# A two-layer graph network on one core: the layout of the degree histogram's one-hots, and how the first feature table is made and handed over

## Chip, cores and metric

One core of a Trainium2 chip. The metric is the device time of one execution in microseconds (us); lower is better. PE is TensorE, DVE VectorE, ACT ScalarE, POOL GpSimd, SP SyncE. PEld is TensorE's loading of weights, which overlaps its matmuls.

## What is computed

12,500 nodes with 32 features and 212,500 edges sorted by destination go through two message-passing layers. The part that the change touches stands ahead of the first layer:

```python
h = jnp.maximum(_layernorm(x, axis=-1), 0.0)
deg_out = jax.ops.segment_sum(ones, src, num_segments=n)
norm_src = jax.lax.rsqrt(jnp.maximum(deg_out, 1.0))
h = features * norm_src[:, None]
msgs = h[src]
agg = jax.ops.segment_sum(msgs, dst, num_segments=n)
```

So each node's outgoing edges are counted, its normalised features are scaled with the inverse root of that count, and layer 1 gathers these scaled rows edge by edge and sums them by destination. Layer 2 computes an edge network (32 to 64 to 256), combines it with gathered node rows and sums again; the change doesn't touch it.

## The kernel before

**Tiling.** Nodes are padded to 12,800 and lie as 128 partitions x 100 rows, in 25 blocks of 4 rows a partition (BLOCKS, BR, NR). Edges are padded to 208 chunks of 1,024, which are 8 tiles of 128 edges. A ring of four buffers (RING) holds the indices (idx) and the gathered rows (g) of four chunks.

**The degree histogram.** Each source node is split in two digits: one of 128 (dig_p) and one of 100 (dig_r), as bfloat16, with an edge tile's 128 edges on the partitions. The 1,664 tiles are taken in 104 batches of HB = 16 tiles. For a batch DVE compares the digits with a constant ramp (iota_p, iota_r) and writes two one-hot arrays (L842 to L852): oh_p holds for each tile 128 flags, oh_r 100 flags. Both are stored with the tile index innermost, 16 tiles side by side, so that one tile's flags lie 16 elements (32 bytes) apart. Each array is written in four pieces (PIECES) that split the 128 or the 100 flags: 8 DVE instructions a batch. TensorE then multiplies, tile by tile, the 128x128 one-hot (as weights) with the 128x100 one-hot and adds up all 1,664 products in one PSUM region (L580 to L591):

```python
mm = pe.matmul(deg, oh_p[:, b, :, t], oh_r[:, b, :, t], start=False, stop=False,
               skip_group_check=True)
```

There are two buffers for the one-hots. DVE waits ahead of batch n until TensorE has signalled the end of batch n-2 (hist_used, L845), and TensorE waits for hist_ready (L582).

**Beside it** POOL gathers rows of the unscaled features for the first 32 chunks (256 indirect DMAs of 128 rows, L445 to L447) and ACT copies them aside (keep, L473). SP loads the indices of the next four chunks as ring buffers come free (load0, L330).

**The table.** When all tiles are counted, DVE takes the inverse root (L861 to L863) and computes hn, the scaled features of all nodes, in one instruction (L864). ACT writes it to DRAM as table1 in one DMA (L486, L487). POOL waits for that (L450) and gathers from it. SP in the meantime has a list of its own (L356 to L371): it waits for bounds_done, the least and greatest destination of each chunk, which DVE reduces after hn (L870, L871); sends these bounds to DRAM and back, broadcast over the partitions; waits for whole_clear; then loads the indices for the first gathers of table1 (load0(EARLY_ITERS - 1), L365); then waits for table1_out and loads a second, local copy of the table (whole, L368, L370).

**After it** DVE clears the accumulator (L874), shifts the destinations (L877) and makes the registers' rows (L880 to L892). Then layer 1 runs: DVE makes a chunk's destination one-hots (L895), TensorE multiplies them with the gathered rows (L600), and DVE adds the sums (L907) when TensorE has signalled. POOL may gather into a ring buffer again when DVE has made the one-hots of a later chunk (used_in, L436).

Of the kernel before, what the change touches and what calls it, by code (L numbers as in the profile page):

```python
# [26 lines left out]
ALU = mybir.AluOpType  # L27
# [6 lines left out]
P = 128  # L34
N_NODES, N_EDGES = 12500, 212500
FEAT, HID, MUL = 32, 64, 8
# [21 lines left out]
EPS = 1e-5  # L58
ALPHA, C110, SI_SCALE = 0.25, 1.0 / np.sqrt(3.0), 1.0 / np.sqrt(float(MUL))
HB = 16  # L60
PIECES = 4
HBATCH = CHUNKS * TILES // HB
EARLY_LINKS = 6
MID_LINKS = 24
MW = 56
# [7 lines left out]
def gnn_program(nc, x_rows, src_all, src_chunks, src_rows, dst_all, dst_chunks, edge_t, sh_chunks,  # L73
                w_l0, b_l0, w1, b1, w2, skip_w, sel_a, sel_b, ident_in, out):
    assert EARLY % RING == 0 and REG_ITERS > A_ITERS + 1
    assert CHUNKS % (2 * HB // TILES) == 0 and CHUNKS % 2 == 0
    with ExitStack() as ctx:
        def sb(name, shape, dt=F32):
# [53 lines left out]
        o = 0  # L132
        dig_p = msg_b[:, :, :, :].rearrange("p b t k -> p (b t k)").bitcast(BF16)[:, 0:T_ALL]
        dig_r, o = hist[:, o:o + T_ALL], o + T_ALL
        oh_p, o = hist[:, o:o + 2 * P * HB].rearrange("p (b j t) -> p b j t", b=2, t=HB), o + 2 * P * HB
        oh_r, o = hist[:, o:o + 2 * NR * HB].rearrange("p (b j t) -> p b j t", b=2, t=HB), o + 2 * NR * HB
        zero_b, o = hist[:, o:o + P], o + P
        early_at = -(-o // 2)
        early = acc_b[:, early_at:early_at + EARLY * TILES * FEAT]
        assert early_at + EARLY * TILES * FEAT <= ACC_W  # L140
        iotas = prod_a[:, :, :, :].rearrange("p b t k -> p (b t k)").bitcast(BF16)
        iota_p = iotas[:, 0:P * HB].rearrange("p (j t) -> p j t", t=HB)
        iota_r = iotas[:, P * HB:(P + NR) * HB].rearrange("p (j t) -> p j t", t=HB)

        dst_i, src_i, src_p, src_b, src_r = (acc_a[:, k * T_ALL:(k + 1) * T_ALL].bitcast(I32) for k in range(5))

# [81 lines left out]
        def by_block(dram):  # L228

            return dram.rearrange("(b p r) f -> p b r f", p=P, r=BR)  # L230
# [79 lines left out]
        def _(sp):  # L310
# [44 lines left out]

            sp.dma_start(early_src, src_rows[0:1, :].to_broadcast([P, CHUNK])).then_inc(early_src_in, 16)  # L356

            sp.wait_ge(bounds_done, 2)
            for k in range(2):
                sp.dma_start(bounds[k:k + 1, :].rearrange("a (q s) -> (a q) s", s=2), mm_c[:, k, :]).then_inc(bounds_out, 16)  # L360
# [1 line left out]
            for k in range(2):  # L362
                sp.dma_start(bound[:, k, :], bounds[k:k + 1, :].to_broadcast([P, CHUNKS])).then_inc(bounds_in, 16)
            sp.wait_ge(whole_clear, 1)
            load0(EARLY_ITERS - 1)  # L365
            sp.wait_ge(table1_out, 16)
            full = GROUPS - 1
            sp.dma_start(whole[:, 0:full, :], table1[0:full * P * GROUP, :].rearrange(  # L368
                "(k p b) f -> p k (b f)", p=P, b=GROUP)).then_inc(whole_in, 16)
# [42 lines left out]
        @block.gpsimd  # L412
        def _(pool):
            pool.iota(iota_all[:, :], [[1, P]], base=0, channel_multiplier=0,
                      allow_small_or_imprecise_dtypes=True).then_inc(iota_done, 1)
            pool.iota(part[:, :], [[1, 1]], base=0, channel_multiplier=1,
                      allow_small_or_imprecise_dtypes=True).then_inc(iota_done, 1)

            def gather(i, table, iteration, free, tiles=TILES):

                for j in range(RING):
                    pool.wait_ge(idx_in[j], 16 * (iteration + 1))
                    free(RING * i + j, j)

                    pool.sem_inc(slots_opened, 1)
                    for t in range(tiles):
                        pool.indirect_dma_start(  # L427
                            out=g[:, j, t, 0:FEAT], out_offset=None, in_=table,
                            in_offset=bass.IndirectOffsetOnAxis(ap=idx[:, j, t:t + 1], axis=0),
                        ).then_inc(gathered[j], 16)  # L430

            def kept_four_before(c, j):

                wait(pool, kept, c - RING + 1)

            def used_in(first_unit, per_iteration, position):  # L436


                def free(i):
                    return lambda c, j: pool.wait_ge(  # L440
                        onehot1_ready, first_unit + per_iteration * i + position[j] + 3)
                return free


            gather(0, x_rows, 0, kept_four_before)  # L445
            with pool.Fori(1, EARLY_ITERS) as i:
                gather(i, x_rows, i, kept_four_before)  # L447


            pool.wait_ge(table1_out, 16)  # L450
            gather(EARLY_ITERS, table1, EARLY_ITERS, kept_four_before)
            beside = used_in(0, len(UNITS), [UNITS.index((0, j)) for j in range(RING)])
            alone = used_in(A_UNITS, RING, range(RING))
            with pool.Fori(0, A_ITERS - 1) as i:
                gather(i, table1, i + (EARLY_ITERS + 1), beside(i))
            gather(A_ITERS - 1, table1, A_ITERS + EARLY_ITERS, beside(A_ITERS - 1), taken(True))
            with pool.Fori(0, REG_ITERS - A_ITERS - 1) as i:
                gather(i, table1, i + (EARLY_ITERS + 1 + A_ITERS), alone(i), taken(True))

            pool.wait_ge(table2_out, 16 * BLOCKS)
            over_iterations(pool, lambda i: gather(
                i, table2, i + ITERS, lambda c, j: wait(pool, d_ready, c - RING + 1)))

        @block.scalar
        def _(act):
# [14 lines left out]
                keep(i)  # L483
            square_root(2)

            act.wait_ge(table1_ready, 1)  # L486
            act.dma_start(by_block(table1), blocks_of(hn)).then_inc(table1_out, 16)  # L487
            keep(EARLY_ITERS - 1)

            def next_sources(e):  # L490
# [81 lines left out]
        def _(pe):  # L572
# [7 lines left out]
            def count(i):  # L580
                for b in range(2):
                    pe.wait_ge(hist_ready, 2 * i + b + 1)  # L582
                    for t in range(HB):
                        mm = pe.matmul(deg, oh_p[:, b, :, t], oh_r[:, b, :, t], start=False, stop=False,  # L584
                                       skip_group_check=True)
                    mm.then_inc(hist_used, 1)

# [176 lines left out]
        def _(dve):  # L764
# [53 lines left out]

            dve.wait_ge(iota_done, 2)
            for iota, m in ((iota_p, P), (iota_r, NR)):  # L820
                link(dve.tensor_copy(iota, iota_all[:, 0:m, None].to_broadcast([P, m, HB])))


            dve.wait_ge(x_loaded, 16)
# [17 lines left out]
            def count(i):  # L842
                for b in range(2):
                    n = 2 * i + b
                    wait(dve, hist_used, n - 1)  # L845
                    for iota, dig, oh, m in ((iota_p, dig_p, oh_p, P), (iota_r, dig_r, oh_r, NR)):
                        for part_m in range(0, m, m // PIECES):
                            rows_m = slice(part_m, part_m + m // PIECES)
                            ins = dve.tensor_tensor(oh[:, b, rows_m, :], iota[:, rows_m, :],  # L849
                                                    dig[:, None, bass.ds(n * HB, HB)].to_broadcast([P, m // PIECES, HB]),  # L850
                                                    ALU.is_equal)
                    ins.then_inc(hist_ready, 1)  # L852

            count(0)
            with dve.Fori(1, HBATCH // 2) as i:
# [5 lines left out]
            link(dve.tensor_scalar(stat[:, 1, :], ps[:, H_BANK, 0:NR], 1.0, None, ALU.max))  # L861
            rsqrt(stat[:, 1, :], norm_src[:, :])
            link(dve.tensor_tensor(norm_src[:, :], norm_src[:, :], stat[:, 2, :], ALU.mult))  # L863
            dve.scalar_tensor_tensor(out=hn[:, :, :], in0=xc[:, :, :], scalar=0.0, in1=rows(norm_src[:, :], FEAT),  # L864
                                     op0=ALU.max, op1=ALU.mult).then_inc(table1_ready, 1)
            dve.memset(whole[:, GROUPS - 1, :], 0.0).then_inc(whole_clear, 1)


# [223 lines left out]
            with dve.Fori(1, A_ITERS) as i:  # L1092
                beside_early(i)
            dve.wait_ge(par_loaded, 16 * N_PARAMS)
            dve.wait_ge(table1_out, 16)
            dve.wait_ge(whole_in, 32)
            link(dve.tensor_copy(split[0], whole))
            link(dve.tensor_tensor(whole, whole, split[0], ALU.subtract))
# [192 lines left out]
```

## Time and profile before

| | us |
|---|---|
| median of three runs | 6182.4 |
| fastest, slowest | 6169.01, 6199.66 |
| the profiled execution's own time | 6176.81 |
| its span (first to last instruction) | 6175.0 |
| PE busy / DVE busy / POOL busy | 3868.4 / 3197.1 / 3114.7 |
| ACT busy | 739.8 |

No engine is busy through the span. The stages in order: start and centring up to about 36 us, the histogram up to 653 us, the table and the bounds up to 690 us, layer 1 up to about 3100 us, layer 2 to the end. A busy share is an average over stages with different limits, so the share of the whole span tells little about the first 690 us. In the views "issue" is idle time that waited for nothing the profile shows, and "remote" is a wait whose releaser the profile does not name.

### The profile page before, as it was taken

To read this page: it belongs to the slowest core of one execution; us is meant where nothing else is said; L and a number is where in the kernel's file an instruction comes from. 1 tells how busy PE (TensorE), PEld (TensorE's weight loads), DVE (VectorE), ACT (ScalarE), POOL (GpSimd) and SP (SyncE) were. 2 spreads that over 40 slices of the span, in tenths; PEclk is the share of its full clock that TensorE was granted. 3 is DMA by queue.
4 is the path that set the end of the run, shared out by engine and by line. 5 is a ranking of instruction groups with operands and counts; after the bars stand their busy time and mean duration, and the time that the engine had idled before them with its cause. 6 is when DMAs were issued, how large, how long until landed. Compare 5 with 4: busy or idle time off the path is not lost.

```text
span 6175.0 us, 73355 instructions
## 1 busy us (share of the span) xinstructions
PE 3868.4 (63%) x19374; PEld 2580.2 (42%) x19375; DVE 3197.1 (52%) x6090; ACT 739.8 (12%) x2428; POOL 3114.7 (50%) x3222
## 2 busy tenths in 40 slices
PE   1069333333455556566667887778877887777877
PEld 0047332332222223222335555555555555555555
DVE  2058432332444334333346666666666766666666
ACT  0000000000000000000022222222222222222222
POOL 7710455555444454455545555554555555555553
PEclk9999955555677777777767787887787777887888
DMA  1100111111000000000001111110111111111110
GB/s 41 16 3 0 37 30 27 29 27 27 20 15 14 14 16 14 14 15 15 15 17 21 20 21 20 20 20 19 21 19 20 21 21 20 21 21 19 20 20 13
DMA packets 237464, 120.99 MB, mean 20 GB/s; under 512 B 148880, under 2 KB 224721, under 8 KB 237329
## 3 DMA queue, kind: packets, MB, share of 16 engines
q0 software_dynamic: 102912, 52.90, 5.9%
q1 hardware_dynamic: 123241, 48.20, 3.3%
q10 hardware_dynamic: 11280, 19.53, 1.0%
q8 instruction: 12, 0.20, 0.0%
q14 instruction: 19, 0.16, 0.0%
HBM read 115.44 MB, written 4.92 MB: 19 GB/s over the span
## 4 chain that ended last, share of the span: by engine, by line
PE 35%; another core or an unknown queue 34%; issue 13%; DVE 11%; DVEq 5%; ACT 2%; ACTq 0%
PE ps L719 11%; PE ps L600 8%; PE ps L707 5%; PE ps L584 5%; PE ps L634 2%; DVEq L912 2%; DVE prod_a L948 2%; DVE prod_a L957 2%; DVEq L911 1%; PE ps L622 1%; PE ps L666 1%; PE ps L753 1%; PE ps L755 1%; ACT q L552 1%
## 5 line engine op out<-in xcount | busy, mean ns | idle before, releaser
L427 POOL DMA_INDIRECT g<-table,idx x2960 | 2855.8, 965 | 2922.0 <-DMA idx<-src_chunks 992.8
L719 PE MATMUL ps<-w_s,hid 128*128 128x256 f32 x3328 | 1084.1, 478 | 353.6 <-ACT hid L540 281.0
L719 PEld LDWEIGHTS ps<-w_s,hid 128*128 128x128 f32 x3328 | 749.4, 237 | 900.9 <-issue 425.4
L907 DVE TENSOR_TENSOR acc_a<-acc_a,ps 33x68 f32 (+1 forms) x416 | 91.4, 220 | 1653.2 <-remote 1448.8
L1152 DVE TENSOR_REDUCE msg_b<-prod_b 128x128 f32<-128x1024 f32 x416 | 828.1, 1991 | 0.0
L634 PE MATMUL ps<-split_s,prod_a 128*128 128x512 bf16 x1568 | 574.7, 452 | 123.1 <-DVE prod_a L948 79.7
L540 ACT ACTIVATE hid<-ps,b_s 64x512 f32<-64x512 f32 x416 | 283.1, 681 | 2321.7 <-remote 1365.2
L707 PE MATMUL ps<-ef,w_s 32*64 32x512 f32 x832 | 527.0, 713 | 45.6 <-issue 42.9
L1136 DVE TENSOR_TENSOR prod_b<-ps,q 128x768 f32<-128x768 f32 x416 | 395.3, 950 | 287.5 <-remote 228.8
L584 PE MATMUL ps<-acc_b 128*128 128x100 bf16 x1664 | 317.7, 371 | 333.6 <-DVE acc_b L849 230.1
L600 PE MATMUL ps<-onehot,g 128*33 128x68 f32 x2816 | 275.9, 271 | 362.9 <-issue 168.5
L600 PEld LDWEIGHTS ps<-onehot,prod_a 128*128 128x128 f32 x3328 | 447.1, 210 | 82.6 <-issue 67.0
L600 PE MATMUL ps<-onehot,prod_a 128*128 128x68 f32 x3328 | 439.9, 290 | 45.6 <-issue 41.0
L600 PEld LDWEIGHTS ps<-onehot,g 128*33 128x33 f32 x2816 | 239.9, 142 | 447.4 <-issue 252.1
L584 PEld LDWEIGHTS ps<-acc_b 128*128 128x128 bf16 x1664 | 239.4, 148 | 411.7 <-DVE acc_b L849 243.2
L600 PE MATMUL ps<-onehot,msg_b 128*56 128x68 f32 x3328 | 289.1, 237 | 194.3 <-issue 193.8
L634 PE MATMUL ps<-xc,prod_a 128*128 128x512 bf16 x784 | 348.1, 444 | 46.3 <-issue 46.3
L552 ACT ACTIVATE q<-g,sh 128x32 f32<-128x32 f32 x1664 | 372.9, 309 | 0.0
L895 DVE TENSOR_TENSOR onehot<-iota_all,dst_rel 128x544 f32<-128x544 f32 x416 | 300.1, 722 | 65.2 <-issue 54.7
L600 PEld LDWEIGHTS ps<-onehot,msg_b 128*56 128x56 f32 x3328 | 239.6, 139 | 217.9 <-issue 202.6
L849 DVE TENSOR_TENSOR acc_b<-prod_a,msg_b 128x512 bf16<-128x512 bf16 x416 | 149.1, 421 | 350.1 <-remote 261.7
L634 PEld LDWEIGHTS ps<-split_s,prod_a 128*128 128x128 bf16 x1568 | 165.1, 111 | 351.1 <-issue 171.6
(127 smaller groups left out, 2949.2 us busy)
## 6 DMA issues: line engine op xcount, KB each, us to landing
g<-table,idx POOLq DMA_INDIRECT x2960
ef<-edge_t SPq DMA_DIRECT2D x208, 128.0 KB
ef<-src_rows ACTq DMA_DIRECT2D x31, 512.0 KB
prod_b<-src_rows SPq DMA_DIRECT2D x112, 64.0 KB
idx<-src_chunks SPq DMA_DIRECT2D x416, 4.0 KB
g<-x_rows,idx POOLq DMA_INDIRECT x256
sh<-sh_chunks SPq DMA_DIRECT2D x208, 16.0 KB
table<-hn ACTq DMA_DIRECT2D x1, 1600.0 KB, 7.3
```

Source lines behind the costliest of these rows:

```text
L427: pool.indirect_dma_start(out=g[:, j, t, 0:FEAT], out_offset=None, in_=table, in_offset=bass.IndirectOffsetOnAxis(ap=idx[:, j, t:t + 1], a ...
L540: act.activation(hid[0:HID, h, :], ps[0:HID, H_BANK + h, :], ACT.Relu, bias=b1_s[:, 0:1]).then_inc(hidden_ready, 1)
L552: act.activation(q[:, j % 2, t, 8:40], g[:, j, t, 0:FEAT], ACT.Copy, scale=sh[:, j, t, 0:1])
L584: mm = pe.matmul(deg, oh_p[:, b, :, t], oh_r[:, b, :, t], start=False, stop=False, skip_group_check=True)
L600: mm = pe.matmul(ps[0:m, S_BANK + b, col:col + WIN], r, oh(t), start=(t == 0), stop=(t == TILES - 1))
L634: mm = pe.matmul(ps[:, R_BANK + b, :], source[:, b, k, :], split[n][:, k, :], start=(k == 0 and n == 0), stop=(k == GROUPS - 1 and n == 2))
L707: pe.matmul(ps[0:HID, H_BANK + h, :], w1_s[32 * j:32 * j + 32, :], ef[32 * j:32 * j + 32, 512 * h:512 * h + 512], start=True, stop=True, t ...
L719: mm = pe.matmul(w_ps[h][:, t, :], hid[:, h, P * t:P * t + P], w2_s[:, :], start=True, stop=True)
L849: ins = dve.tensor_tensor(oh[:, b, rows_m, :], iota[:, rows_m, :], dig[:, None, bass.ds(n * HB, HB)].to_broadcast([P, m // PIECES, HB]), A ...
L895: dve.tensor_tensor(onehot[:, b, :, :], iota_all[:, None, 0:WIN].to_broadcast([P, TILES, WIN]), dst_rel[:, bass.ds(c * TILES, TILES)][:, : ...
L1136: dve.tensor_tensor(prod_b[:, h, :, 0:3, :].rearrange("p t m (i o) -> p t m i o", o=MUL), w[:, :, 128:192].rearrange("p t (i o) -> p t i o ...
L1152: dve.tensor_reduce(msg_b[:, b, 4 * h:4 * h + 4, 0:32].rearrange("p t (g o) -> p t g o", o=MUL), prod_b[:, h, :, :, :].rearrange("p t g (i ...
```

## The change

Three things are edited. One: the one-hots keep their 16 tiles a batch, but as four groups (QUADS) of QUAD = 4 tiles, with only the four tiles innermost; a tile's flags are now 4 elements (8 bytes) apart. The four DVE instructions for an array split the tiles and not the flags, and the ramps shrink to 4 copies of each value. Two: hn is computed in five instructions of 5 blocks each, ACT writes each part with a DMA of its own, and the waits for table1_out are for all five. Three: SP's load0(EARLY_ITERS - 1) moves ahead of the wait for the bounds.

```diff
-PIECES = 4
+QUAD = 4
+QUADS = HB // QUAD
+TABLE_PARTS = 5
+PART_BLOCKS = BLOCKS // TABLE_PARTS
-        oh_p, o = hist[:, o:o + 2 * P * HB].rearrange("p (b j t) -> p b j t", b=2, t=HB), o + 2 * P * HB
+        oh_p, o = hist[:, o:o + 2 * P * HB].rearrange("p (b q j t) -> p b q j t", b=2, q=QUADS, t=QUAD), o + 2 * P * HB
...
-        iota_p = iotas[:, 0:P * HB].rearrange("p (j t) -> p j t", t=HB)
+        iota_p = iotas[:, 0:P * QUAD].rearrange("p (j t) -> p j t", t=QUAD)
...
+            load0(EARLY_ITERS - 1)
             sp.wait_ge(bounds_done, 2)
...
             sp.wait_ge(whole_clear, 1)
-            load0(EARLY_ITERS - 1)
-            sp.wait_ge(table1_out, 16)
+            sp.wait_ge(table1_out, 16 * TABLE_PARTS)
...
-            act.wait_ge(table1_ready, 1)
-            act.dma_start(by_block(table1), blocks_of(hn)).then_inc(table1_out, 16)
+            for k in range(TABLE_PARTS):
+                part_b = slice(k * PART_BLOCKS, (k + 1) * PART_BLOCKS)
+                act.wait_ge(table1_ready, k + 1)
+                act.dma_start(by_block(table1)[:, part_b, :, :], blocks_of(hn)[:, part_b, :, :]).then_inc(table1_out, 16)
...
-                        mm = pe.matmul(deg, oh_p[:, b, :, t], oh_r[:, b, :, t], start=False, stop=False,
+                        mm = pe.matmul(deg, oh_p[:, b, t // QUAD, :, t % QUAD],
+                                       oh_r[:, b, t // QUAD, :, t % QUAD], start=False, stop=False,
                                        skip_group_check=True)
...
-                        for part_m in range(0, m, m // PIECES):
-                            rows_m = slice(part_m, part_m + m // PIECES)
-                            ins = dve.tensor_tensor(oh[:, b, rows_m, :], iota[:, rows_m, :],
-                                                    dig[:, None, bass.ds(n * HB, HB)].to_broadcast([P, m // PIECES, HB]),
-                                                    ALU.is_equal)
+                        for k in range(QUADS):
+                            ins = dve.tensor_tensor(
+                                oh[:, b, k, :, :], iota,
+                                dig[:, None, bass.ds(n * HB + k * QUAD, QUAD)].to_broadcast([P, m, QUAD]),
+                                ALU.is_equal)
...
-            dve.scalar_tensor_tensor(out=hn[:, :, :], in0=xc[:, :, :], scalar=0.0, in1=rows(norm_src[:, :], FEAT),
-                                     op0=ALU.max, op1=ALU.mult).then_inc(table1_ready, 1)
+            for k in range(TABLE_PARTS):
+                part_r = slice(k * PART_BLOCKS * BR, (k + 1) * PART_BLOCKS * BR)
+                dve.scalar_tensor_tensor(
+                    out=hn[:, part_r, :], in0=xc[:, part_r, :], scalar=0.0,
+                    in1=norm_src[:, part_r, None].to_broadcast([P, PART_BLOCKS * BR, FEAT]),
+                    op0=ALU.max, op1=ALU.mult).then_inc(table1_ready, 1)
```

The other waits for table1_out (L451 on POOL, L1095 on DVE) are changed in the same way, and oh_r and iota_r as oh_p and iota_p.

## Rows read from the trace of the kernel before

**Rows 1.** The page's slices: busy tenths of the span in 40 slices

```profile
PE   1069333333455556566667887778877887777877
DVE  2058432332444334333346666666666766666666
```

**Rows 2.** Stretches: length, busy us of PE, PEld, DVE, ACT, POOL, clock, DMA share, GB/s

```profile
36.00:372.00 336.00, 36.44 (x183) 26.17 (x184) 31.48 (x100) 10.84 (x26) 231.37 (x237) 1.00 0.09 14
372.00:653.00 281.00, 281.00 (x1483) 213.27 (x1482) 232.40 (x733) 0.00 (x0) 0.00 (x0) 1.00 0.00 0
```

**Rows 3.** Instruction groups from 372 to 653: busy us, mean ns, idle before

```profile
L584 PE MATMUL ps<-acc_b 128*128 128x100 bf16 x1483 | 281.6, 371 | 0.0
L584 PEld LDWEIGHTS ps<-acc_b 128*128 128x128 bf16 x1481 | 213.3, 148 | 67.7 <-DVE acc_b L849 10.4
L849 DVE TENSOR_TENSOR acc_b<-prod_a,msg_b 128x512 bf16<-128x512 bf16 x365 | 130.8, 421 | 45.5 <-PE ps L584 45.5
L849 DVE TENSOR_TENSOR acc_b<-prod_a,acc_b 128x400 bf16<-128x400 bf16 x368 | 109.8, 362 | 0.0
```

**Rows 4.** Waits from 40 to 372: us in total, times, longest

```profile
DVE acc_b L849 <- remote: 261.7, 8, 43.7
```

**Rows 5.** Timeline from 338 to 371: start, us, engine, line, idle before

```profile
338.15 1.43 DVE L849 TENSOR_TENSOR acc_b<-prod_a,msg_b 128x512 bf16<-128x512 bf16 x4 [41.66 <-remote]
...
340.03 0.94 POOL L427 DMA_INDIRECT g<-x_rows,idx  x1 [0.30 <-issue]
...
340.76 3.21 PE L584 MATMUL ps<-acc_b 128*128 128x100 bf16 x16 [41.00 <-DVE acc_b L849]
368.16 1.43 DVE L849 TENSOR_TENSOR acc_b<-prod_a,msg_b 128x512 bf16<-128x512 bf16 x4 [27.45 <-remote]
...
370.61 1.43 DVE L849 TENSOR_TENSOR acc_b<-prod_a,msg_b 128x512 bf16<-128x512 bf16 x4
```

**Rows 6.** Timeline, DVE: the second batch after 370 and the last

```profile
374.14 1.43 DVE L849 TENSOR_TENSOR acc_b<-prod_a,msg_b 128x512 bf16<-128x512 bf16 x4 [0.99 <-PE ps L584]
...
647.40 1.43 DVE L849 TENSOR_TENSOR acc_b<-prod_a,msg_b 128x512 bf16<-128x512 bf16 x4 [0.38 <-PE ps L584]
```

**Rows 7.** Line L590: weights and matmul on adjacent elements, ns

```profile
L590 PEld LDWEIGHTS ps<-acc_b x1: 127/127/127, 652.9 to 652.9; 128*128 128x128 bf16 x1
L590 PE MATMUL ps<-acc_b x1: 263/263/263, 653.1 to 653.1; 128*128 128x100 bf16 x1
```

**Rows 8.** the one-hots of layer 1 and 2 on DVE: busy us, mean ns

```profile
L895 DVE TENSOR_TENSOR onehot<-iota_all,dst_rel 128x544 f32<-128x544 f32 x416 | 300.1, 722 | 65.2 <-issue 54.7
```

**Rows 9.** Timeline from 653 to 676: the table, SP's list, the first gather

```profile
656.34 3.49 DVE L864 SCALAR_TENSOR_TENSOR hn<-xc,norm_src 128x3200 f32<-128x3200 f32 x1
659.86 0.45 ACTq L487 DMA_DIRECT2D table<-hn  x1
...
668.38 10.78 DVE L874 MEMSET acc_a<- 128x12868 f32 x1 [2.75 <-issue]
668.81 0.84 SPq L363 DMA_DIRECT2D xc<-bounds  x2
669.76 1.78 SPq L334 DMA_DIRECT2D idx<-src_chunks  x4
671.59 0.43 SPq L368 DMA_DIRECT2D acc_b<-table  x1
...
675.41 0.95 POOL L427 DMA_INDIRECT g<-table,idx  x1 [334.44 <-DMA idx<-src_chunks]
```

**Rows 10.** DMA issue of the table: KB, us to landing

```profile
table<-hn ACTq DMA_DIRECT2D x1, 1600.0 KB, 7.3
```

**Rows 11.** Timeline: an early gather, then layer 1's first sums

```profile
14.05 4.22 POOL L427 DMA_INDIRECT g<-x_rows,idx  x1 [0.30 <-issue]
...
689.29 2.02 PE L600 MATMUL ps<-onehot,g 128*33 128x68 f32 x16 [35.90 <-DVE onehot L895]
...
731.54 0.22 DVE L907 TENSOR_TENSOR acc_a<-acc_a,ps 33x68 f32 x1 [33.27 <-remote]
```

More of the change, by code:

```diff
@@ L75, in gnn_program @@
     assert EARLY % RING == 0 and REG_ITERS > A_ITERS + 1
+    assert BLOCKS % TABLE_PARTS == 0
     assert CHUNKS % (2 * HB // TILES) == 0 and CHUNKS % 2 == 0
@@ L134, in gnn_program @@
         dig_r, o = hist[:, o:o + T_ALL], o + T_ALL
-        oh_p, o = hist[:, o:o + 2 * P * HB].rearrange("p (b j t) -> p b j t", b=2, t=HB), o + 2 * P * HB
-        oh_r, o = hist[:, o:o + 2 * NR * HB].rearrange("p (b j t) -> p b j t", b=2, t=HB), o + 2 * NR * HB
+        oh_p, o = hist[:, o:o + 2 * P * HB].rearrange("p (b q j t) -> p b q j t", b=2, q=QUADS, t=QUAD), o + 2 * P * HB
+        oh_r, o = hist[:, o:o + 2 * NR * HB].rearrange("p (b q j t) -> p b q j t", b=2, q=QUADS, t=QUAD), o + 2 * NR * HB
         zero_b, o = hist[:, o:o + P], o + P
@@ L141, in gnn_program @@
         iotas = prod_a[:, :, :, :].rearrange("p b t k -> p (b t k)").bitcast(BF16)
-        iota_p = iotas[:, 0:P * HB].rearrange("p (j t) -> p j t", t=HB)
-        iota_r = iotas[:, P * HB:(P + NR) * HB].rearrange("p (j t) -> p j t", t=HB)
+        iota_p = iotas[:, 0:P * QUAD].rearrange("p (j t) -> p j t", t=QUAD)
+        iota_r = iotas[:, P * QUAD:(P + NR) * QUAD].rearrange("p (j t) -> p j t", t=QUAD)
         dst_i, src_i, src_p, src_b, src_r = (acc_a[:, k * T_ALL:(k + 1) * T_ALL].bitcast(I32) for k in range(5))
@@ L447, in _ @@
                 gather(i, x_rows, i, kept_four_before)
-            pool.wait_ge(table1_out, 16)
+            pool.wait_ge(table1_out, 16 * TABLE_PARTS)
             gather(EARLY_ITERS, table1, EARLY_ITERS, kept_four_before)
@@ L820, in _ @@
             for iota, m in ((iota_p, P), (iota_r, NR)):
-                link(dve.tensor_copy(iota, iota_all[:, 0:m, None].to_broadcast([P, m, HB])))
+                link(dve.tensor_copy(iota, iota_all[:, 0:m, None].to_broadcast([P, m, QUAD])))
             dve.wait_ge(x_loaded, 16)
@@ L1094, in _ @@
             dve.wait_ge(par_loaded, 16 * N_PARAMS)
-            dve.wait_ge(table1_out, 16)
+            dve.wait_ge(table1_out, 16 * TABLE_PARTS)
             dve.wait_ge(whole_in, 32)
```

## The prediction

> **What bounds the kernel now.** I read the page's slices first [rows 1]: PE is nearly idle in slice 1, close to idle in slice 2, then full to slice 4. So the first tenth of the span has stages of its own, and the change lies wholly in it. Then the stretches [rows 2]. From 36 to 372 us the histogram hardly runs: 11% of PE, 9% of DVE, while POOL is busy with gathers. From 372 to 653 us POOL is silent and PE is busy for all 281.0 us, DVE for 232.4. Then the groups of that second stretch [rows 3]: PE's matmuls have no idle time before them, while DVE waited 45.5 us for PE. 368 instructions of the 400-element kind are 92 batches (batch 12 to 103), so only 12 of 104 ran before. Then who waits in the first stretch [rows 4]: DVE, 261.7 us in 8 waits, for a releaser that is not named. The timeline shows how it looks [rows 5]: a batch at 338.15 after 41.66 us idle, the last gather at 340.03, the batch's matmuls from 340.76, and the next batch only at 368.16, with the one after it 2.45 us later. By the code DVE waits there for one thing, TensorE's hist_used, so that signal arrives tens of us after the recorded matmuls while the gathers run. The same is seen in layer 1: a matmul group is recorded at 689.29, the sum of the next is added at 731.54 after 33.27 us of "remote" [rows 11]. So there are two histogram stages: one set by late signals beside the gathers, one set by PE.
>
> **PE in the dense stretch.** The second batch starts at 374.14, the last at 647.40 [rows 6], 90 periods: 273.26 / 90 = 3.036 us a batch, 190 ns for each of its 16 pairs of weights and matmul. The same shapes on adjacent elements take 263 ns for the matmul and 127 ns for the weights [rows 7]; strided they take 371 and 148 [rows 3], 108 and 21 ns more. Taking the excess off, a pair would need 82 ns, but not less than its weights: between 82 and 127. That is for adjacent elements; 4 elements apart may be anything up to today's 190. At 127 a batch takes 2.03 us on PE; at any pair under 154 ns PE is no longer the bound, since DVE needs 2.45 us.
>
> The trace has no matmul that reads at 8 bytes. The Trainium skill, "SBUF — State Buffer" (Door 1, the note on cachelines), says that a read runs at full rate if each line is hit at least twice, which 8 bytes does and 32 doesn't. By that a pair would be near the lower end; the sum is the same, as DVE then paces.
>
> **DVE.** The eight instructions keep their number and size (512 and 400 elements). Unconstrained they take 2.45 us a batch (368.16 to 370.61, [rows 5]). I take 2.45 as unchanged, 2.46 with some register work. The upper bound is that DVE loses the rate at which it takes two bfloat16 a cycle: float32 one-hots of 544 elements cost 722 ns [rows 8], against 421 for 512 here, a slope near 1.04 ns an element from the 3,200 elements in 3.49 us [rows 9]. At one a cycle 512 cost about 689 and 400 about 572, so 268 and 210 more, times four each: 1.91 us a batch, 4.37 in all. I take the unchanged value: every operand still has adjacent elements innermost, as in the rows of 421 ns.
>
> **The sum there.** Batch 12 starts at 370.61; with 91 periods of 2.46 the last starts at 594.5 in place of 647.40: 52.9 us. After its start come DVE's 2.45 and PE's 16 pairs, 2.0 in place of 3.0: 1.0 more. **Minus 54.** PE's lighter load may let its granted clock (1.00 in this stretch, the 2.4 GHz level) drop; what that would cost is in the second rival. The smaller ramps are made while DVE waits for x: nothing, and a few tenths of a us without that cover.
>
> **Beside the gathers** (36 to 368 us) nothing that the change touches holds the signal back, so I count zero. But when the last late signal arrives is luck: it came 27 us after POOL's last gather; the batches there come some 44 us apart (41.66 idle and 2.6 work), so it could come anywhere from 341 to about 382. Bounds: minus 27 to plus 14.
>
> **The table in five parts.** hn takes 3.49 us, issued at 656.34; the DMA is issued at 659.86 and lands 7.3 later, at 667.2 [rows 9, 10]. In five parts the first DMA goes at 657.1; if the bytes set the time all are there at 664.4, if the last part does, no earlier than 660.1 plus its own landing. 2.8 us earlier. Four more instructions cost DVE 4 x 0.07 (337 ns from start to start for 512 elements at two a cycle leave 70): 0.3 us, on the chain that makes the registers' rows. ACT's four more issues, 0.45 each, fit between the parts; its last four copies of gathered rows come behind them and are wanted 30 us later. **Plus 0.3.**
>
> **The index loads.** POOL's first gather of the table starts at 675.41, released by an index that SP issued at 669.76, behind the bounds' second trip at 668.81 [rows 9]. Moved ahead, the four loads have only to wait for gathers that end near 342, so they are long done; SP stands idle there and nothing queued behind it is wanted before bounds_done at 664.7. POOL then starts with the table, at 664.4: 11.0 us earlier. How much of it reaches the end? The first sums start at 689.29 when DVE's one-hots are done, not when the rows are, and DVE's chain (the 10.78 us memset on it) stays. But afterwards the gathers are a ring ahead. And they now meet SP's whole-table load (671.59), as the first gathers met x at 14.05, where one took 4.22 instead of 0.94 us; two such cost some 6 us. Bounds: 0 and minus 11. I take the middle, **minus 5**.
>
> **Forecast.** 6176.8 (the profiled execution) - 54 + 0.3 - 5 = 6118. The median of the runs is 5.6 above that execution, so 6124 against 6182. What this measurement can tell from no change is about 0.5%, 31 us.
>
> **Rivals.** *DVE loses its pace* (slower). Place: the eight compares, whose digit operand now repeats a row of 4 elements in place of 16. It decides as soon as a batch takes DVE over 3.04 us, that is 24% more; at its bound of 4.37 each of 92 batches is 1.33 us longer: +122, less 5, about 6300. For it: no row shows so short a bfloat16 run. Against: the element count and adjacency are as before. 7%.
>
> The Trainium skill, "Vector Engine (DVE) Microarchitecture Reference" (section 5.2), says that a port keeps its full rate only for runs of at least two adjacent 4-byte words that start on an 8-byte boundary; a run of 4 bfloat16 is exactly two words, and its table gives 1.30 in place of 1.054 ns for runs that start on an odd word. No row here shows it. As a mechanism of this kernel, in rows: if the digits start off such a boundary, each compare's 267 and 207 ns of streaming could grow by up to the share by which DVE still beats PE, 24% of the batch, and the 54 us shrink towards zero: 6177, no change. 6%.
>
> *PE keeps 190 ns a pair*, because 8 bytes is as slow as 32, or because a slower clock takes back what the stride gives. Then only the table's part is left: 6177, no change. Against: the 108 ns of excess have no other visible cause. 5%.
>
> *The late signals go away*, because TensorE's strided reads cause them. Then the 104 batches take 104 x 2.46 = 256 us and end near 292; POOL is ready for the table at 342 in place of 675.41, so the rest comes some 330 us earlier: about 5850. Against: in layer 1 the operands are adjacent and the signal is as late [rows 11]. 4%.
>
> **How the numbers follow.** The forecast's case gets 78%. Its own range: 54 + 11 + 27 = 92 us of gain on one side, 54 - 14 = 40 on the other, so 6090 to 6142; with the spread of the three runs (17 us up, 13 down) 6076 to 6158. That holds about 74 of the 78, and the two no-change cases reach into it in part, so the range is 6074 to 6160. Faster by over 0.5% (under 6151): 74 of the forecast's case, 4 of the last rival and 3 from partial losses, 0.81. Within 0.5%: the other 4 of the forecast's case and 8 of the no-change cases, 0.12. Slower: the first rival, 0.07.
>
> **What would show it.** From 372 on, DVE without idle time and batches 2.46 us apart; PE idle between batches, matmuls near 263 ns in place of 371; L590 near 599 us. DVE's compares still 421 and 362 ns: if they are near 690, the first rival. Five issues on ACT 0.7 us apart, and POOL's first gather of the table some 8 us after hn starts, not 19. It is wrong if PE is still full, if a batch's compares are longer, or if the stretch up to the last gather looks different from today's.

## The result, and the profile after

| | before, us | after, us |
|---|---|---|
| median of 7 runs each | 6174.57 | 6113.72 |
| lowest, highest | 6157.22, 6199.66 | 6081.94, 6137.69 |
| profiled execution | 6176.81 | 6112.91 |

The ratio after to before is 0.9897, with a 95% interval of 0.9871 to 0.9922: faster by 0.8 to 1.3%. Forecast were 6124 us, a range of 6074 to 6160, and 0.81 for faster; the gain between the medians was forecast as 58 us and measured as 60.9.

The page's slices of the changed kernel (tenths of the span, 40 slices) answer to [rows 1]:

```profile
PE   0046233333555565666668777777778778788877
DVE  2069332332444343433456766666667566666676
```

PE stood at 6 and 9 in the third and fourth slice and now stands at 4 and 6; DVE has risen from 5 and 8 to 6 and 9: the two have changed places in the dense stretch. The stretches say the same (length, busy us of PE, PEld, DVE, ACT, POOL, clock, DMA share, GB/s), against [rows 2]:

```profile
36.00:372.00 336.00, 19.95 (x192) 17.18 (x192) 32.62 (x105) 10.82 (x26) 230.31 (x236) 1.00 0.09 14
372.00:600.00 228.00, 152.76 (x1473) 131.43 (x1473) 225.54 (x736) 0.29 (x1) 0.00 (x0) 1.00 0.00 0
```

The first stretch is as it was: some 12 batches, DVE at 10%, POOL with its gathers. The second is 53 us shorter, PE is busy for two thirds of it, and DVE for 225.54 of 228.00 us. The granted clock is 1.00 (2.4 GHz) in both stretches, as it was. The groups of that stretch, against [rows 3]:

```profile
L590 PE MATMUL ps<-acc_b 128*128 128x100 bf16 x1472 | 152.7, 273 | 72.7 <-DVE acc_b L855 72.7
L855 DVE TENSOR_TENSOR acc_b<-prod_a,msg_b 128x512 bf16<-128x512 bf16 x364 | 132.1, 445 | 0.0
L590 PEld LDWEIGHTS ps<-acc_b 128*128 128x128 bf16 x1472 | 131.3, 126 | 94.1 <-DVE acc_b L855 94.1
L855 DVE TENSOR_TENSOR acc_b<-prod_a,acc_b 128x400 bf16<-128x400 bf16 x364 | 110.9, 387 | 0.0
```

A matmul lasts 273 ns instead of 371, a load of weights 126 instead of 148. The idle time is what tells who paces: before, DVE had 45.5 us of it, all for PE; now DVE has none and PE has 72.7, all for DVE. The waits from 40 to 372 us (total, times, longest) against [rows 4]:

```profile
DVE acc_b L855 <- remote: 215.2, 6, 42.9
...
DVE acc_b L855 <- issue: 85.2, 2, 43.1
```

The late signals are still there; "issue" stood at 42.8 us in 2 waits before, so the two kinds of wait add up to 304.5 us before and 300.4 now, with 3.0 more for PE. The timeline (start, us, engine, line, idle before) shows the dense stretch's first batches, against [rows 5]:

```profile
366.98 1.43 DVE L855 TENSOR_TENSOR acc_b<-prod_a,msg_b 128x512 bf16<-128x512 bf16 x4 [17.01 <-remote]
...
369.44 1.43 DVE L855 TENSOR_TENSOR acc_b<-prod_a,msg_b 128x512 bf16<-128x512 bf16 x4
...
371.89 1.43 DVE L855 TENSOR_TENSOR acc_b<-prod_a,msg_b 128x512 bf16<-128x512 bf16 x4
```

```profile
372.03 1.66 PE L590 MATMUL ps<-acc_b 128*128 128x100 bf16 x16 [0.80 <-DVE acc_b L855]
```

A batch every 2.45 us, 1.66 of it PE's (104 ns a pair of weights and matmul, where it was 190), then 0.80 of idle. The timeline of the end and of the table answers to [rows 6, 7, 9]:

```profile
592.34 1.48 DVE L855 TENSOR_TENSOR acc_b<-prod_a,msg_b 128x512 bf16<-128x512 bf16 x4
...
596.47 0.26 PE L597 MATMUL ps<-acc_b 128*128 128x100 bf16 x1
...
599.68 3.77 DVE L873 SCALAR_TENSOR_TENSOR hn<-xc,norm_src 128x640 f32<-128x640 f32 x5
600.54 4.01 ACTq L493 DMA_DIRECT2D table<-hn  x5
...
608.35 0.76 SPq L365 DMA_DIRECT2D bounds<-mm_c  x2
608.57 1.49 POOL L431 DMA_INDIRECT g<-table,idx  x1 [268.83 <-DMA table<-hn]
610.37 0.94 POOL L431 DMA_INDIRECT g<-table,idx  x1 [0.30 <-issue]
...
612.00 10.78 DVE L885 MEMSET acc_a<- 128x12868 f32 x1 [2.75 <-issue]
612.55 0.38 SPq L372 DMA_DIRECT2D acc_b<-table  x1
...
632.95 1.34 PE L607 MATMUL ps<-onehot,g 128*33 128x68 f32 x10 [36.22 <-issue]
```

The histogram's last matmul starts at 596.47 instead of 653.12. The first gather of the table now waits for the table and no longer for an index: it starts 8.89 us after hn (608.57 - 599.68), where it took 19.07 (675.41 - 656.34, [rows 9]). The first sums start 36.48 us behind the last histogram matmul, where it was 36.17 (689.29 - 653.12).

### The profile page after: what moved, and what is told of

Read it like the earlier page. It is cut to its first block, busy times and chain, and to the rows that moved or that the text cites. A ratio compares the mean times of both kernels' runs of the same rounds, so it can differ in the third digit from the quotient of the medians.

```text
span 6111.1 us, 73975 instructions
## 1 busy us (share of the span) xinstructions
PE 3727.6 (61%) x19374; PEld 2495.9 (41%) x19375; DVE 3190.0 (52%) x6094; ACT 739.3 (12%) x2428; POOL 3115.5 (51%) x3222
## 4 chain that ended last, share of the span: by engine, by line
PE 34%; another core or an unknown queue 31%; issue 14%; DVE 13%; DVEq 5%; ACT 2%; ACTq 0%
PE ps L726 12%; PE ps L607 9%; PE ps L714 6%; PE ps L641 3%; DVE acc_b L855 3%; DVEq L923 2%; DVE prod_a L959 2%; DVE prod_a L968 1%; DVEq L922 1%; PE ps L629 1%; PE ps L673 1%; ACT hid L546 1%; PE ps L760 1%; PE ps L762 1%
## 5 line engine op out<-in xcount | busy, mean ns | idle before, releaser
L726 PE MATMUL ps<-w_s,hid 128*128 128x256 f32 x3328 | 1070.9, 475 | 368.0 <-ACT hid L546 318.6
L1147 DVE TENSOR_TENSOR prod_b<-ps,q 128x768 f32<-128x768 f32 x416 | 395.5, 951 | 304.5 <-remote 248.4
L607 PE MATMUL ps<-onehot,prod_a 128*128 128x68 f32 x3328 | 447.2, 293 | 45.6 <-issue 41.2
L590 PE MATMUL ps<-acc_b 128*128 128x100 bf16 x1664 | 172.6, 273 | 422.0 <-DVE acc_b L855 256.9
L590 PEld LDWEIGHTS ps<-acc_b 128*128 128x128 bf16 x1664 | 148.5, 126 | 446.0 <-DVE acc_b L855 279.8
L855 DVE TENSOR_TENSOR acc_b<-prod_a,msg_b 128x512 bf16<-128x512 bf16 x416 | 150.8, 442 | 303.4 <-remote 215.2
```

The source lines that it names most:

```text
L590: mm = pe.matmul(deg, oh_p[:, b, t // QUAD, :, t % QUAD], oh_r[:, b, t // QUAD, :, t % QUAD], start=False, stop=False, skip_group_check=True)
L607: mm = pe.matmul(ps[0:m, S_BANK + b, col:col + WIN], r, oh(t), start=(t == 0), stop=(t == TILES - 1))
L726: mm = pe.matmul(w_ps[h][:, t, :], hid[:, h, P * t:P * t + P], w2_s[:, :], start=True, stop=True)
L855: ins = dve.tensor_tensor(oh[:, b, k, :, :], iota, dig[:, None, bass.ds(n * HB + k * QUAD, QUAD)].to_broadcast([P, m, QUAD]), ALU.is_equal)
L1147: dve.tensor_tensor(prod_b[:, h, :, 0:3, :].rearrange("p t m (i o) -> p t m i o", o=MUL), w[:, :, 128:192].rearrange("p t (i o) -> p t i o ...
```

## The experiments

Eight variants and the changed kernel itself were run, three of the variants a second time. The chips they ran on fall into two kinds, and no number below can be read without this: on some, the kernel before takes 6175 to 6261 us, and the traces show the late signals of [rows 4]; on others it takes 4252 to 4257 us, and no variant's histogram shows any there (the kernel before itself was not profiled on such a chip). Times are compared with the kernel before on the same chip. The first three, and the first run of the fourth, were on a chip of the second kind (kernel before: median 4257.41, 13 runs).

**The layout alone** (layout_only). The one-hots as in the change, the table in one part, the index loads where they were; against the changed kernel:

```diff
-TABLE_PARTS = 5
+TABLE_PARTS = 1
...
-            load0(EARLY_ITERS - 1)
             sp.wait_ge(bounds_done, 2)
...
             sp.wait_ge(whole_clear, 1)
+            load0(EARLY_ITERS - 1)
```

> The kernel before with the new layout of the one-hots alone. If the layout carries the gain: batches of the dense stretch 2.45 us apart, the end of the histogram 54 to 57 us earlier than before, the whole time 50 to 60 us under before (about 6120). If instead a good part came from the table's hand-over or from luck with the late signals: 30 us or less.

4214.46 us against 4257.41, ratio 0.9893, interval 0.9877 to 0.991: 43 us, where 50 to 60 were expected for a chip with late signals. Its timeline, at the histogram's end and where the gathers pass from x to the table:

```profile
295.30 1.66 PE L590 MATMUL ps<-acc_b 128*128 128x100 bf16 x16 [0.84 <-DVE acc_b L855]
...
296.78 0.26 PE L597 MATMUL ps<-acc_b 128*128 128x100 bf16 x1
...
313.74 23.64 SPq L338 DMA_DIRECT2D idx<-src_chunks  x4
...
334.75 0.94 POOL L431 DMA_INDIRECT g<-x_rows,idx  x1 [0.31 <-issue]
335.99 0.95 POOL L431 DMA_INDIRECT g<-table,idx  x1 [0.30 <-issue]
```

The whole histogram runs at 2.50 us a batch beside the gathers and ends at 296.78, before the gathers do, and 57 us earlier than with the old layout (353.84, parts_only below). POOL goes from one source to the other without a pause, with SP's loads still in the old place.

**The table in five parts alone** (parts_only), against the kernel before:

```diff
+TABLE_PARTS = 5
...
-            act.dma_start(by_block(table1), blocks_of(hn)).then_inc(table1_out, 16)
+            for k in range(TABLE_PARTS):
+                act.dma_start(by_block(table1)[:, part_b, :, :], blocks_of(hn)[:, part_b, :, :]).then_inc(table1_out, 16)
```

> The kernel before with hn made and written in five parts alone. Expected: all five parts landed about 3 us earlier after the end of the histogram than the one DMA, the compute stretch 0.3 us longer, POOL's first gather of the table still released by the index load, at the same distance from the end of the histogram (22.3 us) as before; whole time as before within its spread. If the parts matter by themselves, that distance shrinks by 3 us or more.

4252.78 us (one run), inside the spread of the kernel before (4248.94 to 4264.68). The table is not what POOL waits for; its first gather comes 20.3 us behind the last histogram matmul:

```profile
353.84 0.27 PE L594 MATMUL ps<-acc_b 128*128 128x100 bf16 x1
...
357.06 3.77 DVE L870 SCALAR_TENSOR_TENSOR hn<-xc,norm_src 128x640 f32<-128x640 f32 x5
357.92 4.02 ACTq L491 DMA_DIRECT2D table<-hn  x5
...
369.84 1.78 SPq L336 DMA_DIRECT2D idx<-src_chunks  x4
...
374.17 0.94 POOL L429 DMA_INDIRECT g<-table,idx  x1 [19.78 <-DMA idx<-src_chunks]
```

**The index loads first, alone** (idx_first_only), against the kernel before:

```diff
+            load0(EARLY_ITERS - 1)
             sp.wait_ge(bounds_done, 2)
...
             sp.wait_ge(whole_clear, 1)
-            load0(EARLY_ITERS - 1)
```

> The kernel before with the index loads ahead of the bounds alone. Expected: POOL's first gather of the table released by the table's DMA, about 14 us after the end of the histogram in place of 22.3; the first sums of layer 1 still at 36.2 us after it, since DVE's chain ends last there; whole time 3 to 8 us under before. If DVE's chain hides it altogether: no difference; if the gathers' start sets layer 1: 8 us or more.

4247.14 us, ratio 0.998, interval 0.997 to 0.9991: a small gain, but one that is there. It is 10.3 us, by the interval 4 to 13, which does not separate the expected 3 to 8 from the case of 8 or more. Here the first gather of the table waits for the table, 15.4 us behind the last histogram matmul, while the first sums of layer 1 start 36.2 us behind it, as before:

```profile
354.16 0.26 PE L590 MATMUL ps<-acc_b 128*128 128x100 bf16 x1
...
360.90 0.45 ACTq L487 DMA_DIRECT2D table<-hn  x1
...
369.51 0.94 POOL L427 DMA_INDIRECT g<-table,idx  x1 [14.82 <-DMA table<-hn]
```

Each of the two parts takes away one of two waits that end close together: the parts alone gain nothing since the index is later; the loads alone leave the one long DMA (8.6 us from its issue at 360.90 to the gather).

**The gathers held until the histogram is done** (gathers_after, and again on another chip of the same kind). This and all that follow are edits of the changed kernel:

```diff
+            pool.wait_ge(degrees_done, 1)
             gather(0, x_rows, 0, kept_four_before)
```

> The changed kernel with POOL's first gathers held back until the histogram is done; nothing is left out. If the gathers hold TensorE's signals back: no late signal, all 104 batches 2.45 us apart, the histogram done near 292 us in place of 596, and the whole time only 20 to 45 us above the changed kernel although nothing overlaps. If the late signals have another cause (an engine's loop, code loading, the start of the program), the first batches crawl as before and the whole time grows by some 300 us.

> The same kernel as gathers_after, for the case that TensorE's signals are late beside GpSimd's gathers (kernel before above 6100 us on the same chip). If they are late only beside the gathers, and for no other reason, the histogram must end within 295 us of the span's start, with no wait of VectorE on a remote signal in it, and then the 236 remaining gathers take 295 us more at 1.25 us each: the first table gather near 615 us, 5 us behind the changed kernel's 609 and thus a time within 20 us of the full change (0 to +20). If something else makes the signals late (the histogram's own matmuls, or the chip as a whole), the histogram is long here too: the first table gather near 900 us and the time 250 us or more above. If the chip is one without late signals, near 4494 us again and nothing is told.

4494.25 us (kernel before: 4257.41) and, again, 4486.37 us (kernel before: 4251.94). The group of its gathers (ns min, median, max; first and last start):

```profile
L431 POOL DMA_INDIRECT g<-x_rows,idx x256: 940/944/3735, 292.3 to 614.3; - x128
L431 POOL DMA_INDIRECT g<-table,idx x64: 940/944/2534, 615.5 to 699.7; - x64
```

The histogram ends at 291 without the gathers, only some 6 us sooner than beside them in layout_only. On these chips the two, with the new layout, hardly hinder each other, and putting them one after the other costs 280 us against layout_only (269 against trailing, below, on the chip of the second run). What the run was to tell of the late signals it could not, since neither chip had them.

The next four kernels ran on a chip with late signals (kernel before: median 6260.71, 8 runs).

**The full change, and the change without the move of the index loads** (full_change, no_idx_move):

```diff
-            load0(EARLY_ITERS - 1)
             sp.wait_ge(bounds_done, 2)
...
             sp.wait_ge(whole_clear, 1)
+            load0(EARLY_ITERS - 1)
```

> The change itself, once more, beside the kernel before on the chip of this call. On a chip like that of the four runs above (before near 4257 us, TensorE's signals not late, POOL gathering without a pause): the layout brings the histogram's end to 297 us, ahead of POOL's last early gather at 335, but SP now stands behind that gather (load0) before it may send the bounds, so DVE's rows and the first sums of layer 1 come after 350 us in place of 348; POOL itself need not wait, so the whole time equals layout_only within 10 us (4205 to 4225). If the queue order costs nothing: under 4212. If the parts or the index loads add a gain of their own: under 4205. On a chip like that of the first result (before near 6175): about 60 us under before.

> The changed kernel with SP's index loads back behind the bounds. On a chip with before near 4257 us: first sums of layer 1 at 348 us as with the layout alone, a few us earlier than the full change; whole time within 5 us of the full change, since POOL sets the end. If SP's order matters to POOL: 8 us or more to one side. On a chip with before near 6175 us: first gather of the table 22 us after the histogram's end instead of 12, whole time up to 10 us above the full change.

6189.67 us, ratio 0.99 (0.9859 to 0.994), and 6207.38 us, ratio 0.9914 (0.9885 to 0.9944). So the full change gains 71 us here, by its interval 38 to 88, where about 60 were expected. The intervals overlap, so the 17.7 us between the medians are not resolved. What the move does at its place: the last histogram matmul and POOL's first gather of the table, in full_change and then in no_idx_move,

```profile
597.28 0.26 PE L597 MATMUL ps<-acc_b 128*128 128x100 bf16 x1
...
609.40 1.49 POOL L431 DMA_INDIRECT g<-table,idx  x1 [268.88 <-DMA table<-hn]
```

```profile
597.09 0.26 PE L597 MATMUL ps<-acc_b 128*128 128x100 bf16 x1
...
617.59 0.94 POOL L431 DMA_INDIRECT g<-table,idx  x1 [277.40 <-DMA idx<-src_chunks]
```

The gather starts 8.2 us earlier with the move, with the histogram's end the same within 0.2 us.

**Eight tiles innermost, flags 16 bytes apart** (quad8):

```diff
-QUAD = 4
+QUAD = 8
```

> The changed kernel with QUAD = 8: one tile's flags 16 bytes apart, half as many DVE instructions, each twice as long. DVE alone would need 2 x 0.60 + 2 x 0.49 = 2.2 us a batch. If what costs TensorE is a new 16-byte line at every element, a pair takes 190 ns again and a batch 3.03 us. If the cost grows with the distance, a pair lies between 104 and 190 ns, and the batch may even be shorter than 2.45 us.

6221.68 us (one run). Its groups from 400 to 600:

```profile
L590 PE MATMUL ps<-acc_b 128*128 128x100 bf16 x1084 | 200.5, 365 | 0.0
L590 PEld LDWEIGHTS ps<-acc_b 128*128 128x128 bf16 x1083 | 157.7, 146 | 42.4
L855 DVE TENSOR_TENSOR acc_b<-prod_a,msg_b 128x1024 bf16<-128x1024 bf16 x136 | 88.0, 689 | 47.0 <-PE ps L590 47.0
```

16 bytes cost TensorE nearly what 32 bytes did (365 against 371 ns, 146 against 148, and 185 against 190 ns a pair), and DVE waits for it again. So nearly all of the layout's gain in TensorE's rate lies between 16 and 8 bytes. The whole time is still 39 us under the kernel before. How these divide is not shown, since the kernel before was not profiled there: the table's two edits are in this kernel, its first gather of the table starts at 651.5 us (full_change: 609.4), and 218 of its histogram matmuls had run by 372 us, against 183 in [rows 2]. The Trainium skill, "SBUF — State Buffer" (Door 1, the note on cachelines), says that a read wants at least two hits in each 16-byte line: flags 8 bytes apart give two, flags 16 bytes apart one. These rows agree with it.

**Two tiles innermost, flags 4 bytes apart** (quad2, and again on a chip without late signals):

```diff
-QUAD = 4
+QUAD = 2
```

> The changed kernel with QUAD = 2: flags 4 bytes apart, 16 DVE instructions a batch of 256 and 200 elements. TensorE's matmul 265 to 273 ns, no better than at 8 bytes if 8 is already free, nearer 263 if not. DVE with its rate kept: 8 x (133 + 70) + 8 x (104 + 70) = 3.0 us a batch, so DVE paces it at 3.0. If rows of two elements break the rate of two a cycle: 8 x 337 + 8 x 278 = 4.9 us a batch, the histogram's end near 545 us, and the mean of the 256-element compare well over its 290 ns.

> The same kernel as quad2, in which one gather took 310 us while the histogram ran without a wait, instead of the histogram waiting while the gathers ran. If that exchange goes with the batches (3.00 us of VectorE against 1.51 us of TensorE, so that the signal is 1.5 us early), it comes again: one gather of about 310 us, no remote wait in the histogram, table gathers from 649 us. If it was chance, the histogram waits for remote signals 200 to 260 us in all, as in the four-tile kernels, and no gather is over 5 us. On a chip without late signals: histogram 312 us beside gathers of 0.94 us, about 4230 to 4250 us.

6279.77 us, inside the spread of the kernel before there (6247.65 to 6281.57), and 4519.16 us on the other chip (before: 4251.94), 267 us slower where 4230 to 4250 us had been expected. The groups of the second from 40 to 340, and then the timeline of the first:

```profile
L431 POOL DMA_INDIRECT g<-x_rows,idx x1 | 310.2, 310159 | 0.3 <-issue 0.3
L855 DVE TENSOR_TENSOR acc_b<-prod_a,msg_b 128x256 bf16<-128x256 bf16 x801 | 169.7, 280 | 0.0
L590 PE MATMUL ps<-acc_b 128*128 128x100 bf16 x1603 | 151.9, 282 | 148.7 <-DVE acc_b L855 148.7
```

```profile
37.15 0.94 POOL L431 DMA_INDIRECT g<-x_rows,idx  x1 [0.30 <-issue]
...
38.40 310.17 POOL L431 DMA_INDIRECT g<-x_rows,idx  x1 [0.30 <-issue]
...
38.72 1.52 PE L590 MATMUL ps<-acc_b 128*128 128x100 bf16 x16 [36.70 <-DVE acc_b L855]
...
348.87 0.94 POOL L431 DMA_INDIRECT g<-x_rows,idx  x1 [0.30 <-issue]
```

One gather takes 310 us, from the end of the first batch of compares to the histogram's end, on both chips, and all others follow after it at 1.25 us each. Meanwhile DVE does 16 compares in 3.00 us without a gap, one each 188 ns. With four tiles innermost it does 8 in 2.50 us (312 ns each), just as gapless, and 201 gathers of 944 ns pass beside them (layout_only). What separates the two is the size and number of DVE's instructions (and with them its innermost rows of two elements in place of four) and the spacing at which TensorE reads. Two gathers ran in 0.94 us beside the first batch of the same compares (35.90 and 37.15), before TensorE's first matmuls at 38.72. So that DVE's instructions hold POOL back is likely and not shown; no run changed one of these alone. The Trainium skill, "SBUF — State Buffer" ("Who interferes with whom"), says that a DVE instruction with two inputs in SBUF contends with a GpSimd instruction that reads SBUF, and that the pair of ports they share is an exclusive lock. The compares have two such inputs, and the gather reads its indices there. The row of 310 us may be that rule, over some 1650 instructions; the unhindered gathers beside the same operation at twice the size show that the rule alone does not tell when it bites.

TensorE's single matmuls read 282 ns, above the 265 to 273 expected, but its 16 pairs take 1.51 us in place of 1.66. DVE, at 3.00 us a batch, hides that.

On the chip with late signals there was a second effect: not one "remote" wait in the whole histogram, from 36 to 349 us, in which only that one gather was under way from 38 us on.

**A matmul behind the signalled one** (trailing, trailing_again):

```diff
                     mm.then_inc(hist_used, 1)
+                    pe.matmul(deg, zero_b, zero_b[:, 0:NR], start=False, stop=False, skip_group_check=True)
```

> The changed kernel with one more matmul (zero stationary, zero moving, added to the degree tile, so nothing changes in it) behind each batch's signalled sixteenth. If TensorE's signal is late because nothing follows the signalled matmul in the queue (it stays behind until TensorE's next instruction), the remote waits in the first 340 us go away or fall under 50 us, the histogram ends near 300 to 350 us and the first table gather is set by the gathers, near 350: some 250 us less than the full change. If it is late because of GpSimd's gathers, the waits stay (200 to 260 us) and the time is within 25 us of the full change, plus nothing for the 104 added matmuls of 0.1 us. On a chip without late signals: within 5 us of the full change's time there (about 4205).

> The same kernel as trailing, for a chip on which TensorE's signals come late (kernel before above 6100 us there). If the signal stays behind until TensorE has its next instruction, the remote waits of VectorE in the first 340 us fall from some 215 to 260 us to under 50 us, the histogram ends by 350 us and the time is some 250 us under the full change (0.99 of before), so near 0.95 of before. If GpSimd's gathers hold it back, the waits stay over 200 us, the histogram ends near 597 us and the time is 0.985 to 0.995 of before. On a chip without late signals: 4217 us again, and nothing is told.

4217.36 and 4208.9 us (kernel before: 4251.94 and 4251.95). Both chips were without late signals, so the question was not answered. The changed kernel itself was not run on such a chip, so these runs, with 104 added matmuls, stand in for it: 0.990 to 0.992 of before, no better than the layout alone (0.9893).

**What adds up.** On chips without late signals POOL's gathers and the issue time between them make 70 to 89% of the chain of waits (60.7% and 24.0% in layout_only), and the time follows the first gather of the table nearly one to one:

| kernel | first gather of the table, us | time, us |
|---|---|---|
| trailing (the full change and a matmul) | 334.6 | 4217.36 |
| trailing_again (the same kernel) | 334.6 | 4208.9 |
| layout_only | 336.0 | 4214.46 |
| idx_first_only | 369.5 | 4247.14 |
| parts_only | 374.2 | 4252.78 |
| gathers_after | 615.5 | 4494.25 |
| gathers_after_again | 615.8 | 4486.37 |
| quad2_again | 643.8 | 4519.16 |

Against layout_only the first column is 33.5, 38.2, 279.5, 279.8 and 307.8 larger further down, the second 32.7, 38.3, 279.8, 271.9 and 304.7. The two repeated kernels differ by 8 us with the same first gather, so one to one holds to about that. So here the histogram's 57 us (353.84 to 296.78) are worth 38, since from there the gathers of x are the later ones.

## Why the prediction was right, point by point

**PE in the dense stretch, DVE.** Right in cause and size. The term was minus 54; the last matmul came 56.65 us earlier. Of these, 1.18 are the last late signal's luck (366.98 instead of 368.16), 53.88 the 92 periods that are now shorter, 1.6 the shorter tail. A pair takes 104 ns (1.66 us for 16, the last one's own tail included), inside the bounds of 82 and 127, and DVE paces at 2.45, as was taken. That a pair needs at least the time of its weights was wrong: one load still reads 126 ns, and the pairs come faster, so the loads overlap. It cost the sum nothing, since DVE paces. The 4.37 us of the first rival did not come. DVE's rows read 445 and 387 ns here instead of 421 and 362, but the starts are as far apart as they were, and in layout_only the same shapes read 418 and 359.

**The rivals.** *DVE loses its pace*: refuted, and by more than was asked, for quad2's rows of two elements keep it too: 256 and 200 elements, eight of each in 3.00 us, where one element a cycle of 1.04 ns (the slope between 544 float32 elements in 722 ns and 3,200 in 3.49 us) would need 8 x (266 + 208) = 3.8 us for the streaming alone. *A run of four off its boundary*: no loss seen, the rate is the unconstrained one; by the code each run starts a multiple of 8 bytes behind its array's start, and where the arrays lie was not read, so a run off the boundary may never have occurred. The Trainium skill, "Vector Engine (DVE) Microarchitecture Reference" (section 5.2), wants runs of two adjacent words for the full rate; quad2's digits are runs of one such word and show no loss, so the measurement decides against that rule for this operand, which repeats its row. *PE keeps 190 ns a pair*: false at 8 bytes, nearly true at 16 (quad8: 185 ns, 1084 matmuls with no idle time before them); and the clock did not fall. *The late signals go away*: false; DVE still waited 215.2 us for them with reads 8 bytes apart.

**Beside the gathers.** Counted as zero, minus 27 to plus 14; measured minus 1.2, and the mix of "remote" and "issue" moved (from 261.7 and 42.8 to 215.2 and 85.2) with no effect on the end of it.

**The table in five parts.** Plus 0.3 for the chain: 3.77 instead of 3.49 us in DVE, and the first sums 0.31 later against the histogram. That it gains nothing alone, since the index is later, is parts_only. The table landed some 8 us after hn began, as forecast (8.9 to the gather).

**The index loads.** POOL's start was to be 11.0 us earlier beyond the histogram's gain; measured 10.2 in the pair of profiles and 8.2 in the pair full_change and no_idx_move, whose table was in five parts both times. The price, minus 5, is the weakest term: the profiled executions differ by 63.9 us, which leaves about 7 behind the 56.65; the medians of the changed kernel with and without the move differ by 17.7, unresolved. On a chip without late signals the move alone gave 10.3 (4 to 13, idx_first_only). So a gain is shown, and that minus 5 was its size is not. One part of its working was wrong: a collision with the whole-table load was priced at two gathers of 4.22 us, and the longest gather there took 1.49. A saying was too broad as well: nothing queued behind the moved loads is wanted early only because the histogram ends long after the last gather of x. In layout_only the order turns, and SP stands in those loads for 23.64 us (313.74) while the whole-table load waits behind them until 337.42. In trailing, which has the move, the bounds stand behind them: SP sends them at 336.21, DVE waits 23.3 us for them, and the first sums start at 356.75 in place of 348.28. The time does not show it, since the gathers set the end there.

**The sum** was 6118 against the profiled 6112.91: of the 5 us missed, 2.65 are the histogram (1.2 of it luck); the other 2.4 can be the index loads or scatter. The room left for luck in the late signals (27 us) was more than they took: the last matmul starts at 596.5, 597.3 and 597.1 in three profiles.

**Open.** Why TensorE's signals come late beside the gathers on some chips and not on others. What the rows show: with gathers, "remote" waits of 176 to 262 us; without them, in the same profiles from 372 on and in quad2, none. Not shown is what holds a signal back, and whether it is TensorE's sending or DVE's receiving; the two kernels meant to tell met no such chip.

Nothing that was tried gives a version better than the changed kernel; on chips without late signals the layout alone is as good as the kernel that stood in for it.

## What to carry to other kernels

Give a bfloat16 matmul operands whose elements lie at most 8 bytes apart, and check both sides of the step: in the same kernel nearly all of TensorE's gain was gone at 16 bytes. Once one engine is relieved, read who paces next from whose idle time is zero, and price the relief only as far as that engine (here 3.04 to 2.45 us, not to PE's 1.66). A smaller innermost run is not always better: with two tiles innermost and a VectorE instruction every 188 ns, one of GpSimd's gathers took 310 us.

## What the runs showed of the hardware

- The same kernel takes 6175 to 6261 us on some chips and 4252 to 4257 us on others. The difference goes with DVE's "remote" waits: on the first kind 261.7 us of them in the first 372, for TensorE's signals, and 1446.5 more at one line of the layers (L907, 690 to 6100); in the histogram on the second kind none, where parts_only's DVE, with the layout of before, waited for PE alone (41.1 of 41.2 us from 40 to 290).
- A GpSimd gather took 310 us beside a gapless row of VectorE's 256- and 200-element bfloat16 compares, on both kinds of chip; beside a gapless row of 512 and 400 (seen on the second kind only) the median was 944 ns.
- A bfloat16 matmul of 128x128 with 128x100 took 371 ns with elements 32 bytes apart, 365 with 16, 273 with 8; a load of its weights 148, 146 and 126.
- Beside the old layout's histogram a gather of x took a median of 1030 ns (237 of them, idx_first_only), beside the new one's 944 (layout_only). That is 18.7 us of the earlier table (353.4 in parts_only to 334.7 for the last gather of x), a gain of the layout on chips without late signals that the prediction did not have. The two rows, idx_first_only and layout_only:

```profile
L427 POOL DMA_INDIRECT g<-x_rows,idx x237: 940/1030/1205, 35.8 to 353.7; - x119
```

```profile
L431 POOL DMA_INDIRECT g<-x_rows,idx x236: 940/944/3482, 35.8 to 334.7; - x118
```
